# Keys and values of three attention layers projected in a stage of their own, kept in DRAM and loaded set by set

## The reference

```
xn = layernorm(x)                              # per layer, from the layer before
q  = xn  @ Wq_l.T + bq_l                       # depends on x
k  = ctx @ Wk_l.T + bk_l                       # depends on the context alone
v  = ctx @ Wv_l.T + bv_l                       # depends on the context alone
p  = softmax over keys of (q . k / sqrt(32))   # per head
x  = x + tanh(g_l) * out_l(p @ v)
```

## Time and profile before

| | |
|---|---|
| median of 3 runs | 3253.7 us (3251.09 to 3257.65) |
| the profiled execution | 3245.69 us, span 3244.0 us |
| mean granted TensorE clock | 0.920 |
| PE, PEld busy | 2705.8 us (83%), 1656.5 us (51%) |
| DVE, ACT, POOL busy | 1725.0 us (53%), 1173.0 us (36%), 918.0 us (28%) |
| HBM read, written | 142.74 MB, 30.67 MB |

### The profile page before, as it was taken

How to read it: one execution, slowest core, us unless ns; L and a number is a source line. 1 busy time by engine, 2 the same in 40 slices (tenths; PEclk the granted TensorE clock), 3 DMA queues, 4 the chain that set the end, 5 groups by cost and what they waited for, 6 DMA issues and landing times. The chain is left out here.

```text
span 3244.0 us, 35880 instructions
## 1 busy us (share of the span) xinstructions
PE 2705.8 (83%) x11495; PEld 1656.5 (51%) x11495; DVE 1725.0 (53%) x3039; ACT 1173.0 (36%) x2506; POOL 918.0 (28%) x436
## 2 busy tenths in 40 slices
PE   7998698999745499999689987588689988599895
PEld 3555586644223366555454543366454543477563
DVE  2453675577665899893655653411555653344212
ACT  0111222566614788781134444111144443221110
POOL 0000000588231010100057663122256663221112
PEclk9989899999977699999799998789799999699998
DMA  6220212422100100100332220432432120212613
GB/s 221 80 95 23 72 67 90 99 70 59 53 30 0 52 27 27 52 26 14 102 70 52 48 59 17 166 113 90 143 70 57 43 59 17 78 39 94 214 65 110
DMA packets 101257, 232.26 MB, mean 72 GB/s; under 512 B 22512, under 2 KB 27120, under 8 KB 99696
## 3 DMA queue, kind: packets, MB, share of 16 engines
q1 hardware_dynamic: 88624, 189.46, 19.5%
q0 software_dynamic: 12480, 40.90, 3.8%
HBM read 142.74 MB, written 30.67 MB: 53 GB/s over the span
## 5 line engine op out<-in xcount | busy, mean ns | idle before, releaser
L1489 POOL TENSOR_TENSOR L_attn_total<-L_attn_total,L_attn_probs 128x2048 f32<-128x2048 f32 x120 | 546.3, 4552 | 152.3 <-ACT L_attn_probs L1444 148.0
L1523 DVE TENSOR_REDUCE L_attn_row_max<-L_attn_rows_ps 128x1 f32<-128x512 f32 x512 | 335.8, 684 | 267.8 <-PE L_attn_rows_ps L1329 264.9
L1444 ACT ACTIVATE L_attn_probs<-L_attn_s_ps 128x512 f32<-128x512 f32 x512 | 292.3, 596 | 418.7 <-PE L_attn_s_ps L1349 414.7
L1349 PE MATMUL L_attn_s_ps<-L_attn_q_stack,L_attn_k_stack 98*128 98x512 f32 (+1 forms) x768 | 378.6, 529 | 39.5 <-DMA L_attn_q_stack<-L_attn_ml 33.5
L436 PE MATMUL L_ffn_hidden<-L_ffn_x_high,L_ffn_up_high 128*128 128x512 f32 x688 | 295.6, 430 | 100.0 <-DVE L_ffn_routes L352 54.2
L318 ACT ACTIVATE L_ffn_sums<-sims 128x128 f32<-128x128 f32 x1024 | 315.5, 390 | 50.3 <-DVE L_ffn_routes L331 26.1
L1489 POOL TENSOR_TENSOR L_attn_total<-L_attn_probs 128x2048 f32<-128x2048 f32 x20 | 91.0, 4552 | 789.2 <-ACT L_attn_probs L1444 789.2
L1349 PEld LDWEIGHTS L_attn_s_ps<-L_attn_q_stack,L_attn_k_stack 98*128 98x128 f32 (+1 forms) x768 | 141.8, 194 | 264.3 <-issue 128.6
L436 PE MATMUL L_ffn_hidden<-L_ffn_x_low,L_ffn_up_high 128*128 128x512 f32 x688 | 272.8, 397 | 0.0
L1362 PE MATMUL L_attn_o_ps<-L_attn_probs,L_attn_values 128*32 128x512 f32 x1536 | 210.8, 621 | 26.4 <-ACT L_attn_probs L1444 22.8
L1329 PE MATMUL L_attn_rows_ps<-L_attn_k_stack,L_attn_q_stack 96*128 96x512 f32 x512 | 207.6, 440 | 29.3 <-DVE L_attn_row_max L1523 27.3
(11 more groups left out here) (272 smaller groups left out, 4227.3 us busy)
## 6 DMA issues: line engine op xcount, KB each, us to landing
L_attn_k_stack<-L_attn_kh SPq DMA_DIRECT2D x192, 128.0 KB, 2.4
L_attn_ctxT<-in_ctxT SPq DMA_DIRECT2D x8, 2048.0 KB, 12.8
L_attn_abs_in<-in_L_ffn_w SPq DMA_DIRECT2D x12, 1024.0 KB, 9.7
L_attn_k_stack<-L_attn_kl SPq DMA_DIRECT2D x96, 128.0 KB, 2.4
L_attn_q_stack<-L_attn_qh SPq DMA_DIRECT2D x192, 64.0 KB, 2.0
L_ffn_xg<-x_slots POOLq DMA_DIRECT2D x46, 256.0 KB, 3.2
y_slots<-L_ffn_y_sb POOLq DMA_DIRECT2D x46, 256.0 KB, 2.3
L_ffn_up_all<-in_L_ffn_w SPq DMA_DIRECT2D x16, 704.0 KB, 13.6
```

The source lines that it names most:

```text
L1349: nc.tensor.matmul(s_ps[:, v % S_SLOTS, :], k_stack[0:depth, n % 2, h, kt * P:(kt + 1) * P], q_stack[0:depth, n % 2, h, :], start=True, st ...
L1444: nc.scalar.activation(probs[:, g % P_SLOTS, h, :], s_ps[:, v % S_SLOTS, :], ACT.Exp, **kinds).then_inc(exp_done, 1)
L1489: nc.gpsimd.tensor_tensor(total[:], first, probs[:, g % P_SLOTS], ALU.add).then_inc(added, 1)
L1523: nc.vector.tensor_reduce(row_max[:, r // HALVES_K, r % HALVES_K:r % HALVES_K + 1], rows_ps[:, r % R_SLOTS, :], AX_X, ALU.max, negate=True ...
```

## The change

- A stage `keys_values_block` behind layer 0's attention output, while the context is still in SBUF. It splits the context (`c_hi`, `c_lo`) and the k and v weights of layers 1 to 3 (`w_hi`, `w_lo`), makes all keys and values with three fp32r matmuls for each fp32 one (high x high, high x low, low x high), splits the keys on the way out, and stores keys (high and low part) and values in DRAM (`keys_scratch`, `values_scratch`). 16 units a layer, each of 12 matmuls for keys and 12 for values, all of 512 columns.
- The attention layers no longer load the context. The norm stage loads the keys and values of sets 0 and 1; later `stack(n)` issues twelve q DMAs, then three DMAs of 512 KB that fill all heads' rows of `k_stack`, then one for the values. A row or a first score now waits for its head's three q DMAs and for all three key DMAs (`k_loaded`).
- `CHUNK_AT` keeps the q item alone (units 12, 14, 16, 18), and only the two q items stand ahead of set 0; set 0's rows stand behind them in one piece, with nothing between.
- GpSimd adds six groups a set (1 to 6) instead of seven; TensorE sums group 7 with four ones-matmuls ahead of its PV. Only set 7 is summed group by group in all layers. `probs` has four slots instead of three.
- The output weights have a tile of their own, and are loaded behind `stack(1)` instead of at the end.

```diff
@@ new stage, called behind the output block of layer 0 @@
+def keys_values_block(env, layers, kd, vd):
...
+            def _(sp):
+                def load_raw(l):
+                    if l:
+                        sp.wait_ge(w_ready, W * l)
+                    sp.dma_start(weights[:, DC:W, :], layers[l]["wk"].rearrange("f p n -> p f n")).then_inc(raw_loaded, 16)
+                    sp.dma_start(weights[:, 0:DC, :], layers[l]["wv"]).then_inc(raw_loaded, 16)
...
+                    for u in range(UNITS):
+                        i = UNITS * l + u
+                        if u % 2:
+                            n, b = u // 4, u // 2 % 2
+                            sp.wait_ge(kl_done, i + 1)
+                            for part in range(2):
+                                sp.dma_start(kd[l, BATCH * n + b, part], staged[:, i // 2 % 2, part, :].bitcast(F32)).then_inc(
+                                    k_stored[i // 2 % 2], 16)
+                        if u % VQ == VQ - 1:
+                            sp.wait_ge(v_done, i + 1)
+                            sp.dma_start(vd[l, u - VQ + 1:u + 1].rearrange("t p n -> p t n"), v_sb[:, i // VQ % 2]).then_inc(
+                                v_stored[i // VQ % 2], 16)
...
+            @block.tensor
+            def _(pe):
+                for l in range(L):
+                    for u in range(UNITS):
+                        i = UNITS * l + u
+                        f, j = u // BLOCKS, u % BLOCKS
+                        pe.wait_ge(w_ready, W * l + DC + f + 1)
+                        if l == 0:
+                            pe.wait_ge(c_ready, min(u, BLOCKS - 1) + 1)
+                        if i >= 2:
+                            pe.wait_ge(kl_done, i - 1)
+                        steps = [(c, w, x) for c in range(DC) for w, x in terms]
+                        for q, (c, w, x) in enumerate(steps):
+                            last = nc.tensor.matmul(k_ps[:, i % 2, :], w[:, f, c * P:(c + 1) * P],
+                                                    x[:, c, j * HALF:(j + 1) * HALF], start=(q == 0), stop=(q == len(steps) - 1))
+                        last.then_inc(k_psum, 1)
+                        if i >= 2:
+                            pe.wait_ge(v_done, i - 1)
+                        for q, (c, w, x) in enumerate(steps):
+                            last = nc.tensor.matmul(v_ps[:, i % 2, :], x[:, c, u * P:(u + 1) * P], w[:, place(l, c), :],
+                                                    start=(q == 0), stop=(q == len(steps) - 1))
+                        last.then_inc(v_psum, 1)
...
+                for j in range(BLOCKS):
+                    nc.scalar.copy(c_hi[:, :, j * HALF:(j + 1) * HALF], env.ctxT[:, :, j * HALF:(j + 1) * HALF]).then_inc(c_high, 1)
+                    if j == 0:
+                        for i in range(W):
+                            split(0, i)
...
+                        nc.scalar.activation(keys_of(0, i, u % 2), k_ps[:, i % 2, :], ACT.Identity,
+                                             bias=bk[:, l, u // BLOCKS:u // BLOCKS + 1]).then_inc(kh_done, 1)
+                        if l + 1 < L and u % 2:
+                            split(l + 1, u // 2)
...
@@ loads of an attention layer @@
+class AttentionInputs:
...
+    def load_keys(self, sp, n):
+        for r, part in enumerate((0, 1, 0)):
+            sp.dma_start(self.k_stack[32 * r:32 * (r + 1), n % 2].bitcast(F32),
+                         self.kd[n, part].rearrange("(h p) k -> p h k", p=32)).then_inc(self.k_loaded[n % 2], 16)
+
+    def load_values(self, sp, n):
+        b, f = n % BATCH, n // BATCH
+        KT = CTX // P
+        sp.dma_start(self.values[:, n % self.V_SLOTS],
+                     self.vd[b * KT:(b + 1) * KT, :, f * P:(f + 1) * P].rearrange("t p e -> p t e")).then_inc(
+                         self.v_loaded[n % self.V_SLOTS], 16)
...
@@ streamed_attention_block @@
-    KEYS, QUERIES, VALUES = (0, 1), 2, (3, 4)
-    TURN, SUMS = 5, 6
+    QUERIES, TURN, SUMS = 0, 1, 2
     less_max_rows = keep_mask is None
-    S_SLOTS, R_SLOTS, P_SLOTS, V_SLOTS = 3 if less_max_rows else 5, 2, 3, 3
-    SUMMED = range(SETS - 1 if less_max_rows else SETS - 2, SETS)
-    EARLY = 5
+    S_SLOTS, R_SLOTS, P_SLOTS, V_SLOTS = 3 if less_max_rows else 5, 2, 4, inputs.V_SLOTS
+    SUMMED = range(SETS - 1, SETS)
+    ADDS = KT - 2
-    CHUNK_AT = {u: (item, c) for item, units in ((3, (0, 1, 3, 4)), (4, (8, 9, 10, 12)), (0, (13, 14, 15, 16)),
-                                                 (1, (17, 18, 20, 21)), (2, (22, 23, 24, 26)))
-                for c, u in enumerate(units)}
-    SPLIT_AT = {max(u for u in CHUNK_AT if CHUNK_AT[u][0] == i) + 1: i for i in range(5)}
-    LOW_AT = {u + (i == QUERIES): i for u, i in SPLIT_AT.items()}
+    CHUNK_AT = {u: (QUERIES, c) for c, u in enumerate((12, 14, 16, 18))}
+    SPLIT_AT, LOW_AT = 19, 20
...
-    FIRST_ITEMS = [(0, 0), (0, 1), (0, 2), (0, 3), (0, 4), (1, 3), (1, 4), (1, 0), (1, 1), (1, 2)]
+    FIRST_ITEMS = [(0, QUERIES), (1, QUERIES)]
...
-                        for dst, parts in ((k_stack, (kh, kl, kh)), (q_stack, (qh, qh, ql))):
-                            for r in range(3):
-                                sp.dma_start(dst[HD * r:HD * (r + 1), s, h, :].bitcast(F32),
-                                             parts[r][HD * h:HD * (h + 1), :].bitcast(F32)).then_inc(stacked[h], 16)
+                        for r, part in enumerate((qh, qh, ql)):
+                            sp.dma_start(q_stack[HD * r:HD * (r + 1), s, h, :].bitcast(F32),
+                                         part[HD * h:HD * (h + 1), :].bitcast(F32)).then_inc(stacked[h], 16)
+                    if n >= 2:
+                        inputs.load_keys(sp, n)
+                    if n >= 3:
+                        sp.wait_ge(pv_done, KT * (n - 2))
+                    if n >= 2:
+                        inputs.load_values(sp, n)
...
+                        pe.wait_ge(inputs.k_loaded[n % 2], KEYS * (n // 2 + 1))
...
+                    if g in summed_groups:
+                        first = kt == (0 if n in SUMMED else KT - 1)
+                        if first:
+                            pe.wait_ge(ones_made, 1)
+                            pe.wait_ge(product_free, place[n, SUMS] - 1)
+                        for h in range(HG):
+                            last = nc.tensor.matmul(bank(n, SUMS)[HD * h:HD * (h + 1), :], ones[:], probs[:, g % P_SLOTS, h, :],
+                                                    start=first, stop=(n in SUMMED and kt == KT - 1))
+                        last.then_inc(summed, 1)
...
-                pe.wait_ge(env.ctx_loaded[0], 16)
-                for n, i in FIRST_ITEMS[:EARLY]:
+                for n, i in FIRST_ITEMS:
                     for c in range(DC):
                         chunk(n, i, c)
-                pe.wait_ge(env.ctx_loaded[1], 16)
-                for j in range(EARLY * DC):
-                    chunk(*FIRST_ITEMS[EARLY + j // DC], j % DC)
-                    if less_max_rows:
-                        for r in range(j * ROWS // (EARLY * DC), (j + 1) * ROWS // (EARLY * DC)):
-                            row(0, r)
+                if less_max_rows:
+                    for r in range(ROWS):
+                        row(0, r)
                 if less_max_rows:
...
-                        if kt and n not in SUMMED:
+                        if 0 < kt < KT - 1 and n not in SUMMED:
```

275 lines of the change are left out of this document (165 added, 110 removed).

## The result

The changed kernel takes 3581.19 us (median of 4 runs, 3577.18 to 3585.96) beside 3255.68 us before on the same chip: a ratio of 1.1002, 95% interval 1.0981 to 1.1023. The profiled execution took 3585.96 us with a span of 3583.9, 339.9 more than before. The predicted 3530 was 51 us too low.

The account below looks back on a forecast made before the run. It took GpSimd's adds to bound layer 1, and the chain of scores, row maxima, exponentials and PV layers 2 and 3. 3245.7 + 285 - 57 + 52 = 3526, median 3534, rounded to 3530; range 3455 to 3610.

Parts of the forecast that it names:

- The stage, +285: New block behind layer 0, between barriers: 1152 matmuls, 261 us, plus lead-in and tail; +285 us (275 to 298).
- Layer 1, -57: Layer 1, paced by GpSimd's adds: earlier start, -21, and shorter sets; -57 us (-65 to -45).
- 27.3 + 3.2 + some 1.6 for the rest = 32.1: Layer 1, us a set: GpSimd's six adds, its wait before the first, and the rest; 32.1 instead of 38.2.
- the 1 us a set that was set aside for the clock: Layer 1: TensorE idles some 6 us a set at the sums; half clock behind that loses 1 us a set.
- 29 for set 6: Layer 1, near its end: set 6 takes 29 us, after five sets of 32.1.
- 25 units of set 7: Layer 1's end: 25 units of set 7 at 1.06 us each, ending at 827 beside 890.2.
- Layers 2 and 3, +26 each: Layers 2 and 3, each: start -5, set 0 -4, sets 1 to 5 +25, set 6 +10.5; +26 us.
- Set 1 to 5: 42.4 + 3 + 10 = 55.4, less 1.4, since some of set 6's own half-clock time falls into the wait: 54: Layers 2 and 3: chain, Q and sums, and 10 us key wait make sets 54 us instead of 49.0, +25.
- (a): Rival, layers 2 and 3: keys land in time, sets take 45.4 instead of 49; median 3406 (3370 to 3430); 10%.
- (b): Rival, layers 2 and 3: half clock spreads over whole sets, 60 us each, +64 a layer; median 3617; 14%.
- (c): Rival, sets 0 to 5 of each layer: TensorE-bound, so all 402 us come off against 285; median 3137; 4%.

Follow-up runs that it names:

- 12: Changed kernel with keys loaded head by head, layer 1's sums ahead of unit 8 instead of 7, and repeated score matmuls in all three layers: 3377.20 us.
- 11: Kernel before the change, with GpSimd adding six groups a set in layer 1 instead of seven and TensorE four more ones matmuls: 3249.71 us, ratio 1.0002.
- 1: Changed kernel with keys loaded head by head, three 128 KB DMAs ahead of the same head's query DMAs: 3398.48 us, ratio 1.0460.
- 3: Changed kernel with a third key stack slot and keys loaded a set ahead, by the same three 512 KB DMAs: 3411.12 us, ratio 1.0495.
- 7: Changed kernel with the new stage run twice in a row: 3864.97 us, ratio 1.1895.
- 2: Changed kernel with twelve unused fp32 matmuls ahead of the first row of each set from 2 on: 3564.39 us, ratio 1.0970.

## Why the prediction was right, and what it missed

**The stage, +285.** Right: 286.9 by the events, of which 1.5 arose ahead of it; TensorE stood idle for 17.0 us ahead of the first matmul, until GpSimd's splits of the weights, and the matmuls are 227 ns apart behind a first fourteen or so at half clock.

**Layer 1, -57 forecast, -42 measured.** The start came out (17.4 us from the block's first matmul to the first exponential, 37.6 before). The sets did not: they gave back 24 us where 36 were forecast. The forecast counts by GpSimd's first adds, and so can the trace:

```profile
903.88 4.53 POOL L1633 TENSOR_TENSOR L_attn_total<-L_attn_probs 128x2048 f32<-128x2048 f32 x1 [4.99 <-ACT L_attn_probs L1589]
1003.74 4.53 POOL L1633 TENSOR_TENSOR L_attn_total<-L_attn_probs 128x2048 f32<-128x2048 f32 x1 [3.18 <-ACT L_attn_probs L1589]
1036.24 4.54 POOL L1633 TENSOR_TENSOR L_attn_total<-L_attn_probs 128x2048 f32<-128x2048 f32 x1 [3.17 <-ACT L_attn_probs L1589]
1071.25 4.52 POOL L1633 TENSOR_TENSOR L_attn_total<-L_attn_probs 128x2048 f32<-128x2048 f32 x1 [5.72 <-ACT L_attn_probs L1589]
```

"27.3 + 3.2 + some 1.6 for the rest = 32.1" was nearly right: the period is 32.5 us where the clock is kept and the wait is 3.2, and with a wait of 4.3 to 5.7 it is 33.7 to 35.0. The five periods from 903.88 to 1071.25 take 167.4 us instead of 160.5, about the 1 us a set that was set aside for the clock. The terms that were too small are the two ends: set 0, 33.0 us instead of 30.8, and above all "29 for set 6" with "25 units of set 7" behind it, 56 us together, where 64.1 lie between 1071.25 and take 7. Between takes 5 and 6 the granted clock is 0.67; in 12, which holds it better and has its sums a unit later, the same stretch takes 59.6. So about half of the 8 us may go with the clock; the rest stays open. That GpSimd paced layer 1 before was only half true, as 11 shows: TensorE did too.

**Layers 2 and 3, +26 each forecast, +41 and +50 measured** with their starts. The mechanism was right in place and kind: the keys stand behind twelve query issues, TensorE is at unit 5 long before they land, one wait a set, all of it gone in 1 and 3. Its size was 12.4 us instead of 10: in the set shown the third transfer landed 8.7 us after its issue where the prediction had 6.3, which is 17.6 us behind the last score of the set before (2086.08) instead of 16, and TensorE stood there after 5.1 us instead of 6. The step that was off is "Set 1 to 5: 42.4 + 3 + 10 = 55.4, less 1.4, since some of set 6's own half-clock time falls into the wait: 54". The chain without products is 40.6 us, not 45.4, and the half clock is added by the wait instead of hidden in it: 40.6 + 12.4 + 5.0 = 58.0. That 54 came so near is luck in part: a chain 4.8 too long stood against a wait 2.4 too short and a half clock 6.4 too cheap. In the sum of a layer set 0 hid more of it: from first exponential to take 0 it gave back 10.3 and 10.7 us where 4 were forecast; sets 1 to 5 cost 42 and 45 more instead of 25, set 6 14 and 20 instead of 10.5. The two layers differ by no more than executions do: in 7, where they are unchanged, they took 419.5 and 429.1 us instead of 413.0 and 422.4. TensorE: Matmul & The Clock Gate of the Trainium skill says, in its section on how the oscillation of the clock bites in real kernels, that a wait on a DMA in every tile lets every tile start at half clock. The trace agrees with 0.61 over the 16 us behind the wait; in 2, with most of the wait filled, the clock still falls in seven of the twelve sets to 0.86 to 0.91.

**The rivals.** (a), keys in time, was put at 3406: kernels 1 and 3, which are that case, gave 3398 and 3411. (b), half clock takes the layers, was put at 3617 (its own terms, 3245.7 + 285 - 57 + 128, make 3602 and 3610 for the median); the result lies between it and the forecast, since the clock took 3 to 5 us of each set beside the wait. (c) needed 285 us given back. Kernel 1 gives back 287 - 149 = 138, and 12 gives back 161, the lighter adds, the shorter starts and 12's repeated scores among it. So of 402 us busy the products cost the kernel before at most some 140 to 160 us where they stood; the rest lay beside maxima, exponentials and adds.

## What to carry to other kernels

Work that fills the gaps of another chain costs its hidden price, not its busy time. Before moving it into a stage of its own, find what the chain takes without it, here 42 us a set beside 48, and compare that with the stage, which pays every matmul in full.

When a load replaces parts that were made in place, ask when its first reader comes, and give each reader its own part and its own wait. Head by head in the same queue, ahead of each head's queries, was worth 5% here.

A lighter TensorE can be a slower one: look at the granted clock of the stretch, and try whether repeated matmuls pay.

## What the runs showed that was not expected

Useless matmuls made the kernel faster: 3389 to 3377 us with 8 to 16 repeated scores a set. A long idle time filled with matmuls but for 3.5 us did not keep the clock: it fell to 0.63 some 25 us later, in a stretch that the records show busy for 9.95 of 11 us (at half clock each record is longer). And a later sum in the kernel before, which shortened one wait of GpSimd from 3.2 to 1.6 us, made the sets in the middle of layer 1 2.7 us longer.
